# Gated delta rule on one Trainium2 core: the triangular inverse from 8x8 blocks instead of from pairs, and two of its copies issued by ScalarE

## The reference

```python
def step(S, xs):                       # one token, S is 128x128 for each head
    qt, kt, vt, gt, bt = xs
    S = S * jnp.exp(gt)[..., None, None]
    kS = jnp.einsum('bhk,bhkv->bhv', kt, S)
    S = S + bt[..., None, None] * kt[..., :, None] * (vt - kS)[..., None, :]
    o = jnp.einsum('bhk,bhkv->bhv', qt, S)
    return (S, o)
...
mixed = _silu(conv)                    # causal convolution of 4 taps over x @ W_qkv
...
o = _gated_delta_rule(q, k, v, g, beta)
o = o * jax.lax.rsqrt(var + 1e-06) * norm_w * _silu(z)
return o.reshape(B, T, value_dim) @ W_out
```

## Time and profile before

| | |
|---|---|
| Time, median of 3 | 3104.99 us (3104.87 to 3106.11) |
| Profiled execution | 3106.92 us, of which the span is 3105.2 |
| Instructions in the span | 120272 |
| TensorE matmul, weight load | busy 92%, 68% |
| VectorE, ScalarE, GpSimd | busy 61%, 53%, 37% |
| Mean granted TensorE clock | 0.975 of full speed |

### The profile page before, as it was taken

How to read it: one execution, slowest core, us unless ns; L and a number is a source line. 1 busy time by engine, 2 the same in 40 slices (tenths; PEclk the granted TensorE clock), 3 DMA queues, 4 the chain that set the end, 5 groups by cost and what they waited for, 6 DMA issues and landing times.

```text
span 3105.2 us, 120272 instructions
## 1 busy us (share of the span) xinstructions
PE 2854.6 (92%) x50586; PEld 2109.6 (68%) x50586; DVE 1899.5 (61%) x4174; ACT 1661.2 (53%) x5196; POOL 1147.7 (37%) x1519
## 2 busy tenths in 40 slices
PE   3399997999999999999999999999999999999995
PEld 2155555777776777777777777777777777777774
DVE  3223324667766677667676677766666666766663
ACT  2111112656665666656666566666666656665662
POOL 0222111444444444444444444444444444443441
PEclk9799998999999999999999999999999999999997
DMA  1522111111111111111111111111111111111111
GB/s 40 152 58 51 24 40 47 41 49 43 50 43 41 37 53 51 34 44 47 46 48 44 43 46 47 47 44 46 46 46 46 46 46 46 46 46 46 46 46 58
DMA packets 225770, 148.90 MB, mean 48 GB/s; under 512 B 187456, under 2 KB 195936, under 8 KB 225120
## 3 DMA queue, kind: packets, MB, share of 16 engines
q1 hardware_dynamic: 219104, 123.56, 13.9%
q0 software_dynamic: 6144, 17.83, 2.4%
HBM read 115.79 MB, written 2.70 MB: 38 GB/s over the span
## 4 chain that ended last, share of the span: by engine, by line
PE 61%; issue 10%; POOL 4%; ACT 3%; DVE 3%; DMA 1%; SPq 1%; POOLq 0%; DVEq 0%; ACTq 0%
PE rps L795 10%; PE rps L728 7%; PE rps L720 6%; PE rps L836 5%; PE rps L845 5%; PE rps L682 4%; PE rps L667 3%; PE rps L699 3%; PE rps L812 3%; PE rps L825 3%; PE rps L692 3%; PE rps L670 2%; PE rps L760 2%; PE rps L769 2%; PE rps L711 2%
## 5 line engine op out<-in xcount | busy, mean ns | idle before, releaser
L1244 DVE SCALAR_TENSOR_TENSOR conv<-rps,w_in,conv 128x509 f32<-128x509 f32 (+2 forms) x768 | 566.9, 745 | 23.3 <-ACT conv L1033 3.9
L795 PE MATMUL rps<-xnT,w_in 128*128 128x512 f32 x1024 | 498.9, 610 | 24.6 <-DVE cols L1226 13.2
L1420 POOL TENSOR_TENSOR decay_b<-decay,beta_k 128x512 f32<-128x512 f32 x128 | 130.4, 1040 | 783.5 <-DVE beta_k L1260 783.5
L947 ACT ACTIVATE upd<-rps 128x256 f32<-128x256 f32 x260 | 99.6, 383 | 423.3 <-PE rps L682 423.3
L720 PE MATMUL rps<-w_outn,gatedT 128*128 128x256 f32 x1056 | 295.8, 406 | 4.0 <-issue 3.1
L795 PEld LDWEIGHTS rps<-xnT,w_in 128*128 128x128 f32 x1024 | 175.3, 191 | 157.3 <-issue 125.2
L728 PE MATMUL rps<-w_z,xnT 128*128 128x256 f32 x1040 | 263.9, 387 | 2.0 <-ACT z L982 2.0
L845 PEld LDWEIGHTS rps<-xq,wq 32*32 32x32 f32 x16384 | 170.5, 105 | 135.7 <-issue 118.2
L1033 ACT ACTIVATE conv<-rps,w_in 128x512 f32<-128x512 f32 x256 | 175.6, 686 | 161.4 <-PE rps L795 161.2
L1296 DVE TENSOR_TENSOR xq<-rps,xq 128x256 f32<-128x256 f32 x256 | 108.7, 425 | 248.7 <-PE rps L845 247.7
L845 PE MATMUL rps<-xq,wq 32*32 32x32 f32 x16384 | 205.1, 194 | 56.9 <-issue 56.6
(11 more groups left out here) (208 smaller groups left out, 6450.3 us busy)
## 6 DMA issues: line engine op xcount, KB each, us to landing
sums_row<-g_rows SPq DMA_DIRECT2D x65, 1024.0 KB, 5.0
scale<-comb_rows POOLq DMA_DIRECT2D x40, 256.0 KB, 5.4
w_in<-in_w_in SPq DMA_DIRECT2D x17, 520.0 KB, 3.4
bq<-bmat SPq DMA_DIRECT2D x256, 32.0 KB, 2.0
inv<-xq SPq DMA_DIRECT2D x256, 32.0 KB
w_z<-in_w_z SPq DMA_DIRECT2D x17, 256.0 KB, 2.8
w_out<-in_w_out SPq DMA_DIRECT2D x17, 256.0 KB, 5.2
invT<-xqT SPq DMA_DIRECT2D x128, 32.0 KB
```

The lines of the kernel that those rows point to most:

```text
L795: last = nc.tensor.matmul(ps[PROJ_BANK[j]][:, :], w_in[:, m * 4 * P + j * P:m * 4 * P + (j + 1) * P], xnT[:, m, b * T:(b + 1) * T], start= ...
L1244: nc.vector.scalar_tensor_tensor(conv[:, j, shift:T], ps[PROJ_BANK[j]][:, 0:T - shift], w_in[:, k:k + 1], conv[:, j, shift:T], ALU.mult, A ...
L1420: nc.gpsimd.tensor_tensor(decay_b[:, us, :], decay[:, us, :], beta_k2[:, us].unsqueeze(2).to_broadcast([P, NC_, C]), ALU.mult).then_inc(db ...
```

## The change

The merge levels for blocks of 2 and 4 and the pairs before them are gone. In their place the inverses of the 8x8 diagonal blocks are computed by substitution: GpSimd masks the 8x8 blocks (`blocks8`), VectorE folds them to 8 columns (`compact`), GpSimd spreads 7 rows of each over a tile of 448 columns (`rows8`), one float32 product with a matrix of ones in 8x8 blocks gives each row to the 8 partitions of its block (`spread_rows`, TensorE), and VectorE runs the substitution (`substitute`: one operation, then six pairs of a product and a difference on 48 to 8 columns, then the 8x8 blocks put into `xq`, then the transpose). ScalarE issues the copies of blocks 0 and 1 of `xq` into `inv` at the end of its step (`expand`), and `solve(0)` waits for them; SyncE issues the other four. All four engines have a new order of calls.

```diff
-LEVELS = (2, 4, 8, 16)
+G = P // 4 // 8
+R = 8
+LEVELS = (8, 16)
 NL = len(LEVELS)
...
-parts = [r == c, r <= c, r > c, np.ones((P, P), bool), rq == cq, merge(1) * -1.0]
-parts += [merge(s) for s in LEVELS]
+parts = [r == c, r <= c, r > c, np.ones((P, P), bool), r // R == c // R]
+parts += [rq // R == cq // R] + [merge(s) for s in LEVELS]
+parts += [rq // R == cq[:, :G], r % R == cq[:, :R]]
...
         after(xqT_done, n(XT) + XT)
         for rows in BLOCKS[:2]:
-            sp.dma_start(invT[rows, :, rows], xqT[rows, :, :]).then_inc(full_in, 16)
-        for rows in BLOCKS:
-            sp.dma_start(inv[p][rows, :, rows], xq[rows, :, :]).then_inc(full_in, 16)
+            sp.dma_start(invT[rows, :, rows], xqT[rows, :, :]).then_inc(half_in, 16)
+        for rows in BLOCKS[2:]:
...
             pe.wait_ge(x64_done, n(1) + 1)
+            pe.wait_ge(inv_in, n(32))
             pe.wait_ge(upd_done, n(4))
...

     pe.wait_ge(x32_done, n(3) + 1)
-    pe.wait_ge(full_in, n(96))
+    pe.wait_ge(half_in, n(64))
     pe.wait_ge(z_done, n(2))
...
+        def spread_rows():
+
+            pe.wait_ge(x0_done, n(2) + 2)
+            pe.wait_ge(gT_done, n(2) + 1)
+            pe.wait_ge(x32_done, n(3) + 3)
+            nc.tensor.matmul(ps[TRI][:, 0:U * (R - 1) * R], cst[:, SAME8:SAME8 + P],
+                             b8_rows[:, :, :, :].rearrange("p u k j -> p (u k j)"), start=True, stop=True).then_inc(b8_ps, 1)
...

             pe.wait_ge(bqs_done, n(NL) + lv + 1)
             pe.wait_ge(xqT_done, n(XT) + lv + 1)
-            if lv == 0:
-                pe.wait_ge(gT_done, n(2) + 1)
...
         join_w(n)
         project(0)
         join_x(n)
+        by_token(1)
+        halves_w(n)
         project(2)
-        halves_w(n)
-        by_token(1)
+        halves_x(n, r)
         gated_transpose(n, 0)
-        halves_x(n, r)
-        pe.wait_ge(tap_done, n(12) + 6)
-        gated_transpose(n, 1)
         k_products(1)
         pe.wait_ge(v_done, n(2))
         solve(0)
-        by_token(0)
         project(3)
         attend(0)
+        pe.wait_ge(tap_done, n(12) + 6)
+        gated_transpose(n, 1)
+        read_state(1)
+        by_token(0)
+        solve(1)
+        k_products(0)
+        attend(1)
+        pe.wait_ge(wz_in, (i + (1 if b == 0 else 2)) * 16)
+        pe.wait_ge(tap_done, n(12) + 12)
+        project_z(tb, 0)
+        read_state(2)
+        project_z(tb, 1)
+        spread_rows()
+        solve(2)
         pe.wait_ge(ksq_done, n(1) + 1)
         pe.wait_ge(kw_done, n(2) + 2)
         project_out(n, 0, loads)
-        read_state(1)
-        k_products(0)
         project_out(n, 1, loads)
-        solve(1)
+        pe.wait_ge(qsq_done, n(1) + 1)
+        project_out(n, 2, loads)
+        attend(2)
         by_token(2)
-        pe.wait_ge(wz_in, (i + (1 if b == 0 else 2)) * 16)
-        pe.wait_ge(tap_done, n(12) + 12)
-        project_z(tb, 0)
-        project_z(tb, 1)
-        attend(1)
         merge_w(0)
-        read_state(2)
+        read_state(3)
         merge_x(0)
-        solve(2)
+        solve(3)
         pe.wait_ge(acc_done, n(2) + 1)
         project_z(tb, 2)
+        attend(3)
+        project_out(n, 3, loads)
         merge_w(1)
-        attend(2)
         project_z(tb, 3)
         merge_x(1)
-        read_state(3)
-        merge_w(2)
-        solve(3)
-        merge_x(2)
-        attend(3)
-        pe.wait_ge(qsq_done, n(1) + 1)
-        project_out(n, 2, loads)
-        merge_w(3)
-        project_out(n, 3, loads)
-        merge_x(3)
         by_token(3)
...
+        def expand():
+
+            act.wait_ge(xqT_done, n(XT) + XT)
+            for rows in BLOCKS[:2]:
+                nc.scalar.dma_start(inv[p][rows, :, rows], xq[rows, :, :]).then_inc(inv_in, 16)
+
         first_tap(1)
         take_join(n)
         first_tap(0)
-        first_tap(2)
+        squares_by_token(1)
         take_halves(n)
         silu(0)
-        squares_by_token(1)
+        first_tap(2)
         take_updates(0)
+        take_transposes(n, 0)
+        first_tap(3)
+        take_transposes(n, 1)
+        take_state_part(1)
+        take_updates(1)
         silu(2)
-        take_transposes(n, 0)
-        take_transposes(n, 1)
-        first_tap(3)
-        take_updates(1)
-        take_state_part(1)
+        exp_decay((b + 1) % BATCH, n(4) + 8, n(2) + 2, 0)
+        take_state_part(2)
+        squares_by_token(0)
         squares(0)
+        take_updates(2)
+        exp_decay((b + 1) % BATCH, n(4) + 8, n(2) + 2, 1)
         silu(3)
         take_merge(0)
-        squares_by_token(0)
-        take_state_part(2)
-        take_updates(2)
         squares(1)
+        take_state_part(3)
+        take_updates(3)
+        squares(2)
+        gate_z(n, 0)
+        squares(3)
         take_merge(1)
-        gate_z(n, 0)
         take_v(0)
         gate_z(n, 1)
-        squares(2)
-        take_state_part(3)
-        take_merge(2)
-        take_updates(3)
-        exp_decay((b + 1) % BATCH, n(4) + 8, n(2) + 2, 0)
-        squares(3)
-        take_merge(3)
-        exp_decay((b + 1) % BATCH, n(4) + 8, n(2) + 2, 1)
         take_v(1)
+        expand()
...
-        def first_transpose():
-
-            dve.wait_ge(x0_done, n(2) + 2)
+        def compact():
+
+            dve.wait_ge(x0_done, n(2) + 1)
+            nc.vector.tensor_reduce(b8[:, :, :], bq8[:, :, :].rearrange("p u (q j) -> p u j q", q=G), AX.X, ALU.add).then_inc(b8_done, 1)
+
+        def substitute():
+
+            b_rows = ps[TRI][:, 0:U * (R - 1) * R].rearrange("p (u k j) -> p u k j", u=U, k=R - 1)
+            unit = cst[:, UNIT8:UNIT8 + R]
+            dve.wait_ge(b8_ps, n(1) + 1)
+            nc.vector.scalar_tensor_tensor(x8[:, :, 1:R], b_rows[:, :, 0, 1:R], neg_first[:, 0:1],
+                                           unit[:, 1:R].unsqueeze(1).to_broadcast([P, U, R - 1]), ALU.mult, ALU.add).then_inc(x8_done, 1)
+            for k in range(1, R - 1):
+                dve.wait_ge(x8_done, n(X8) + 2 * k - 1)
+                nc.vector.tensor_tensor(t8[:, :, k + 1:R], b_rows[:, :, k, k + 1:R],
+                                        x8[:, :, k:k + 1].to_broadcast([P, U, R - 1 - k]), ALU.mult).then_inc(x8_done, 1)
+                dve.wait_ge(x8_done, n(X8) + 2 * k)
+                nc.vector.tensor_tensor(x8[:, :, k + 1:R], x8[:, :, k + 1:R], t8[:, :, k + 1:R], ALU.subtract).then_inc(x8_done, 1)
+            dve.wait_ge(x8_done, n(X8) + 2 * R - 3)
+            dve.wait_ge(x32_ps, n(1) + 1)
+            dve.wait_ge(w64_ps, n(1) + 1)
+            nc.vector.tensor_tensor(xq[:, :, :].rearrange("p u (q j) -> p u q j", q=G),
+                                    x8[:, :, :].unsqueeze(2).to_broadcast([P, U, G, R]),
+                                    cst[:, BLOCK8:BLOCK8 + G].unsqueeze(1).unsqueeze(3).to_broadcast([P, U, G, R]),
+                                    ALU.mult).then_inc(x8_done, 1)
+            dve.wait_ge(x8_done, n(X8) + 2 * R - 2)
             nc.vector.transpose(xqT[:, :, :], xq[:, :, :]).then_inc(xqT_done, 1)

...
         gating(n, 0)
-        gating(n, 1)
         taps(1)
         join(n, r)
         taps(0)
+        k_beta()
+        gating(n, 1)
+        halves(n, r)
         taps(2)
-        halves(n, r)
-        k_beta()
-        decayed_k(0)
-        decayed_k(1)
         b_of_head(0)
         b_of_head(1)
         new_state(0)
         output(0)
         residual(1)
         taps(3)
-        add_out(n, (b - 2) % BATCH, 0)
-        first_transpose()
         new_state(1)
         output(1)
+        compact()
         residual(2)
-        merge(0)
+        decayed_k(0)
+        decayed_k(1)
+        substitute()
         new_state(2)
         output(2)
-        merge(1)
+        add_out(n, (b - 2) % BATCH, 0)
         residual(3)
         scores_of_head(0)
-        merge(2)
+        merge(0)
+        scores_of_head(1)
         output(3)
-        scores_of_head(1)
         add_out(n, (b - 2) % BATCH, 1)
-        merge(3)
+        merge(1)
...
-        def pairs():
+        def blocks8():

             pool.wait_ge(diag_in, i * (64 * BATCH) + 64 * (b + 1))
-            pool.wait_ge(x32_ps, n(1) + 1)
-            pool.wait_ge(w64_ps, n(1) + 1)
-            masked(bq1, MERGE1).then_inc(x0_done, 1)
-            pool.wait_ge(x0_done, n(2) + 1)
-            nc.gpsimd.tensor_tensor(xq[:, :, :], bq1[:, :, :], cst[:, IDQ:IDQ + Q].unsqueeze(1).to_broadcast([P, U, Q]),
-                                    ALU.add).then_inc(x0_done, 1)
+            pool.wait_ge(b8_done, n(1))
+            masked(bq8, IN8).then_inc(x0_done, 1)
+
+        def rows8():
+
+            pool.wait_ge(b8_done, n(1) + 1)
+            pool.wait_ge(b8_ps, n(1))
+            nc.gpsimd.tensor_tensor(b8_rows[:, :, :, :], b8[:, :, :].unsqueeze(2).to_broadcast([P, U, R - 1, R]),
+                                    cst[:, UNIT8:UNIT8 + R - 1].unsqueeze(1).unsqueeze(3).to_broadcast([P, U, R - 1, R]),
+                                    ALU.mult).then_inc(x0_done, 1)

```

(54 more changed lines are left out.)

## The result

Five runs of the changed kernel have a median of 3090.0 us (3088.03 to 3094.3), those of the kernel before, on the same chip, 3104.87 (3099.33 to 3106.11). The ratio is 0.9958, 95% interval 0.9943 to 0.9972: 13 us or 0.4% faster, where 195 us were forecast. The direction was right, the size was wrong by a factor of 15, and 3090 lies outside the range of 2865 to 2980.

A forecast was written before the change was run, and what follows sets the result against it. TensorE's own queue was taken as the bound. Per step 34.5 queue + 1.35 head wait + 0.3 near misses + 0.25 gaps = 36.4 us, 3.05 less, x 64 = 195 us: 2910 us, own range 2870 to 2940, wider range 2865 to 2980.

The forecast's parts named there:

- Its reduction: TensorE's queue per step: merges take away 3.75 us, spread_rows adds 0.8, net -2.95, so 37.45 becomes 34.5 us.
- The spread_rows product: On TensorE, one float32 product over 448 columns: 0.75 us, 0.8 with its start.
- The substitution: VectorE behind spread_rows: 15 dependent operations and the transpose, 3.9 us, covered by some 4.4 us of TensorE work.
- Near misses: Paths within half a microsecond of each other, such as GpSimd's masks to rows8: 0.3 us a step, bounds 0 and 1.
- The gaps at merge_x: TensorE's "issue" gaps, read as instructions not yet arrived: 0.25 us a step left of 1.7 to 2.0, bounds 0 and 1.8.
- the rivals that half stays or all do: Gaps at merge_x: half stays, 0.9 us a step, 2952 us, chance 0.14; or all, 1.8, 3009 us, chance 0.10.
- is busy about 80% of the loop: Sign expected in the profile after: VectorE's busy share of the recurrent loop, about 80%.
- The wait at the head of the step: TensorE's by_token(1) waits for ScalarE's silu(1), starting at 6.35 instead of 5.0: 1.35 us a step, bounds 0.85 and 4.0.
- VectorE's total: VectorE's work per step: 27.0 less two merges of 0.87 plus about 3.5 gives 28.8 of 36 us, below TensorE's queue.
- at some 12.5: Start of solve(0) on TensorE, in us after project(1) starts; the copies ScalarE issues until 2.6 would be early.
- VectorE becomes the bound: Rival, behind spread_rows: small operations cost 0.3 not 0.2 us, TensorE waits 0.75 to 1.0 more, about 2965 us; chance 0.13.
- The move of the copies: Two copies issued by ScalarE instead of SyncE: whole effect 0.5 us at the head of the step (1.35 against 0.85).

The follow-up runs named there:

- gate_early_sp: gate_early, but SyncE issues all six copies again and ScalarE none: 2862.71 us, ratio 0.9253 to the kernel before.
- gate_early_2: The kernel of gate_early run once more, unchanged, as base of the second set: 2928.61 us, ratio 0.9466 to the kernel before.
- gate_early: The changed kernel with VectorE's gating(1) moved back directly behind gating(0), nothing else moved: 2925.95 us, ratio 0.9471 to the kernel before.
- pool_waits: The changed kernel, VectorE's order kept, but GpSimd waits for gating(1) before decays_by_beta(0): 2936.78 us, ratio 0.9489 to the kernel before.
- gate_psum: The changed kernel, but gating(1) reads PSUM in place of z (result not the reference's) and TensorE waits for it before attend(0): 2923.92 us, one run.
- token_late_sp: gate_early with by_token(1) behind project(2) and halves_w, gated_transpose(0) before halves_x, take_halves before squares_by_token(1), SyncE issuing all six copies: 2849.0 us, ratio 0.9202.

## Why the prediction was wrong

**What held.** The bound before: TensorE's queue. Its reduction: an undisturbed step of 37.45 us of queue was to become 34.5; in gate_early_sp, which has the change's order of TensorE, it is 34.2. The spread_rows product costs 0.75 us (1720.78 to 1721.53). The substitution, forecast at 3.9 us, takes from 1721.73 to the end of the transpose at 1725.68, 3.95, and merge_w(0) waited for it 1.4 us in the whole run. rows8 took 0.96. Near misses, forecast at 0.3 a step, came to (6.5 + 1.4) / 64 = 0.12. The gaps at merge_x went from 56.6 to 12.6 us, 0.2 a step are left, where 0.25 was taken; the rivals that half stays or all do fell. The cause is not shown: that these are instructions that hadn't arrived remains an inference, only that with two thirds of the instruction bytes most are gone. One sign came true by luck: VectorE "is busy about 80% of the loop". It is 2024.8 us of 2511, 81%, but as 31.6 us in a step of 39.2 and not as 28.8 of 36. The wait at the head of the step was 70.6 / 64 = 1.10 and not 1.35, because the issues on ScalarE lie partly beside the last take_v.

**The step that failed** is the paragraph that put VectorE's total at "27.0 - 2 merges of 0.87 + about 3.5 = 28.8 of 36. Its queue stays below TensorE's", and with it solve(0) "at some 12.5". It took every duration of VectorE from where it stood before, and asked of the new order only what waits for what. But the length of gating depends on what GpSimd does beside it. The change put gating(1) right behind k_beta, whose second last operation is what releases decays_by_beta, so that the two start together each step, and it put log_decays right behind. That made 1.1 us into 4.26. halves came 3.2 us later, and solve(0) waited 2.03 a step. No term and no rival of the prediction held it: the rival "VectorE becomes the bound" looked behind spread_rows, where nothing happened. Apart from gating the term was sound: in gate_early_2 VectorE is busy 2003.8 us, 104 more than before, where 115 were forecast (although "about 3.5" leaves out `compact`, 0.59 us a step).

**The second omission** is the clock. The sum took waits as costing their own length. In this case longer waits went with stretches of 0.50: by the estimate the change lost 121 us to the clock and the kernel before 78 (0.025 x 3105.2, of which some 25 in the loop, at 0.99), 43 more.

**A term too large** is the one for gaps. The sum lets 2.0 us a step of "disturbed" time shrink to 0.25, a gain of 1.75 x 64 = 112 us. The named waits that went are 44 us at merge_x and 20 for GpSimd's masks and taps(1), 64 in all. The 56.6 us of merge_x were 0.9 a step; the rest of the 2.0, as far as the rows show it, was other waits and the lower clock, of which only those 20 us went.

**The account.** Added to the forecast, for the profiled execution:

| | us |
|---|---|
| Queue of TensorE, 64 x -2.95 | -189 |
| Gaps at merge_x, 56.6 to 12.6 | -44 |
| GpSimd's masks and the wait for taps(1), gone | -20 |
| Head of the step, by_token(1) | +71 |
| spread_rows and merge_w(0) | +8 |
| solve(0), behind gating(1) | +128 |
| Clock, 78 to 121 | +43 |
| Sum | -3 |
| Measured, span 3105.2 to 3092.6 | -13 |

The first line is the forecast's own; with the 34.2 of gate_early_sp it is -207 and the sum -21. The measured value lies between.

The large change moved the time little because 152 us (gate_early_2 against the change) went into one collision and what followed from it. The 71 us at the head of the step had been forecast. That the collision was the cause is shown by three kernels that avoid it in three ways: gate_early, pool_waits and gate_psum (one run) all lie between 2924 and 2937 us. By the ratio of gate_early_2 the change without the collision would take 0.9466 x 3104.87 = 2939 us here, 29 above the forecast of 2910 and inside its own range; so most of the miss is this one step.

**The move of the copies** was said to have its "whole effect" at the head of the step, 0.5 us, 32 us in all. The direction held in all four comparisons. The place held too: the wait there shrank by 25 us in gate_early_sp. But the clock behind that wait went with it, so the size ran from 9 us, in the kernel before, to 66 in gate_early.

## What to carry to other kernels

Before an operation is moved, look at what the other engines do at its new place. Here a VectorE operation with two wide SBUF inputs kept its length while GpSimd was idle, or when one of the two inputs was in PSUM, and otherwise lasted as long as GpSimd's operation. A wait that has no releaser in the profile is settled by reading the code's waits and then the timeline of each engine that they name; here the sign was a line whose mean had doubled (353 ns to 722). Price a wait on TensorE at more than its length when it comes each step: of the 66 us between gate_early_2 and gate_early_sp the wait itself was 25. A new order that removes a wait has a price of its own, 0.6 us a step in token_late_sp, so compare the undisturbed steps as well.
